# Taking thinned neighbours out by indirect writes into ranked rows, in a two-layer graph kernel

## The chip, the cores and the metric
One core of a Trainium2 chip runs the whole program. The time is device microseconds of that core, lower is better. TensorE, VectorE, ScalarE, GpSimd (POOL in the profile) and SyncE (SP, which here only issues DMAs) each follow their own instruction list and meet at semaphores.

## The reference, cut to what matters
```python
# x (16, 1024, 64) f32, adj (16, 1024, 1024) f32, sparse with heavy hubs; nodemask all true
h = relu(layernorm(x));  x = x + (adj / clip(adj.sum(2), 1)) @ h          # layer 0
h = relu(layernorm(x))                                                    # layer 1
neigh = (adj > 0) & ~eye;  nb = neigh.sum(-1)
rank = cumsum(neigh, -1) - neigh                       # which neighbour of its row
skip = where(nb > 10, (nb + 1) // 2, 1)
rem = neigh & (skip > 1) & (rank % skip == skip - 1) & mask[:, :, None]
rem = rem | rem.T                                      # taken out on both sides
nd = where(eye, 1, adj) with rem set to 0, > 0;  nv = nd.sum(2)
s = sort(where(nd[..., None], h[:, None], inf), axis=2)
agg = sum of w * (quantile tau of the nv sorted values), tau in (.25, .5, .75)
x = x + (relu((h + agg) @ W1 + b1) @ W2 + b2) * mask
```
A row with more than ten neighbours loses at most two of them (the neighbours of rank skip-1 and 2*skip-1), and each loss is taken over into the neighbour's own row. In the inputs that the reference draws, each of the 16 graphs has 44 to 52 nodes with more than ten neighbours, and the largest node has 78.

## The kernel before, in words
The 16 graphs go in 8 pairs (g, b). For each graph the kernel

- streams the transposed adjacency in eight pieces (`adl`, tile AT, ring of 3), makes 0/1 masks of it on VectorE (`nei`, NEIT) and multiplies it for layer 0 on TensorE (`msg`, psL, line 557);
- counts neighbours by matmuls with a triangular matrix (`cum`, line 568) and writes a signed rank code per entry into VR on ScalarE (line 841): for a neighbour a small positive number, for a non-neighbour a negative one. VR is one buffer of eight 128-row tiles, so the next graph's codes wait until this graph's rows have left it;
- thins (`thin` on POOL, `abs` on ScalarE, `rem` on VectorE): POOL works out two target ranks for every row, ScalarE writes |code - middle| into RM (line 848), VectorE turns it into -4096 where it hits a target (line 1169);
- adds VR, RM and RM transposed in PSUM (`sc`, function `codes`, lines 589 to 596), and ScalarE writes the sum through Relu back into VR (line 867): an entry that was taken out becomes 0. ScalarE then counts the row's valid entries by the sum of signs (`cn`, line 873);
- sorts the nodes by neighbour count (`cls`, `key`) and writes each VR row with its features to its rank's place in `rows` in device memory (`sca`, 8 indirect DMAs by POOL, line 1505).

For each pair it then reads the ranked rows back in tiles of 128 (`ldr`, tile RR), turns them (`pos`, `turn`, tiles POSA and POSB), makes one-hot matrices on VectorE (`gd`, OHB, lines 1194 to 1209), gathers the neighbours' features on TensorE (`gm`, psG, lines 651 and 660), sorts them on VectorE (`cmp` on W, `bat` on HUB, lines 1227 to 1277; for HUB ScalarE moves a share), weighs and adds them, and does the two dense products (`f1`, `f2`) and the output (`out`, 16 indirect DMAs). Ranks 0 to 127 are the hubs.

The order in which all this is issued is a string, ORDER, one letter per step kind; each engine walks the same list of steps and does its part of each. A step's place in the string so sets its place in every engine's queue. Graphs with a node of more neighbours than its slots hold go a slow way (`ov`), which is skipped where a flag is 0.

Of the kernel before, what the change touches and what calls it, by code (L numbers as in the profile page):

```python
# [28 lines left out]
    "XnnnUUUAAMMUWUMMAADDRMDDAUUUADDDDMDAAMWDDDTDDDUDMDDRUUMATABBBBBMUBBBMrANAgrrrrrrrNNMUssckWUssssAccss"  # L29
    "cSSSSRMssssccssUUsASMsccDDDSSSMAAhDlDMDWRDDDDDDDNNNDDDDDXThnBBnUUUTnBBBAAgMUBrBBArrrrrrMMrssUcksssAf"  # L30
    "UcssMcscsssscsssWScSSSRsAccMLMDDAUUAASSSSDDFLDUDDDWDDDDDMDDDDDTTFFMRLLBBBBFrrBFFgUUBBBMMLLMFFrrArrrr"
    "fksFAssssssssslddsVVAccmNmddNccmmvdNdUMeWLULsmmSAevdUdAUmdGmdeeFFFLLmdsSommccesdhSSFFmSRddsKKKKsKKcc"
    "MAFMDDlDDDLUDKLSSSMDDDAAmmWDDDDeeTKddQBBMKBBmmDRUUUKDDDDdmNQrdQdeFTFBFBLLNBBmmtXQQdFFQQmFgrrrerQLLQr"
    "rrANssssssdndcenmknsssSssAFFFQWcccttMMptssscmUepssUMMdAcdcmmSSQScAUAtDDQSSSSpDLLDDRtdAdDDDmmtMDteUUt"
    "FFFeLLMtpUAAMMtWFFFpLDLDDDDJJpRJFFFTUUAMJJGtDADDDThtBMBadUBdffMlABBBBBULLMrmmrNrrddmderrrrFmQUFQtFms"
    "AesgddtssAssLssLNkccccWmsssQQNVVAtmdshSmeesQSSSddRtstQsvMQtMtttttttsttUtcUccpmmMAAddcMlSQQpFFSSSFeRm"
    "UUXUDDDDDQDmQQWDDDDDDQQNDddANNDEDDLLmmTDDeddeETEnvmmddFFEnAmmgtBBoFnderkdEAEMmMBBBBBBrrrrErmEeLUrrUL"
    "sssesssccKKKKKKMMcsssssdcdEFFFpcmUSSSSssssWRttAMAtcLLscmpMcUAttKMUDDSSStSMAAUDDDeFFFELLKddQWKKmDDDDD"
    "DDDEFQRQDDtFFQQDDDdmQQdmTmTtUQQBBhBAUAlLLBBMUFFFBrBBNrQAgQMrMrQtrrrrLLQeeUUFFFNtJMOkssssssJLLpOssJNJ"
    "ssssccJddcQtsmmQteQSSdccmWdSSmASAAdGGdRtsmmchcQddpttDDDMDQtttUAUttssAtcMMMQtSSStDtlWRetfefpmtttmpXeF"  # L40
# [1630 lines left out]
```

## Time and profile before
| | |
|---|---|
| median of 3 runs | 1417.88 us (1410.16, 1417.88, 1423.46) |
| span of the profiled execution | 1381.6 us |
| TensorE matmul busy | 1209.3 us, 88% |
| VectorE busy | 1129.0 us, 82% |
| ScalarE busy | 958.9 us, 69% |
| GpSimd busy | 734.6 us, 53% |

The profiled execution's own time is not shown beside its span; the span lies 28.6 us below the fastest of the three runs and 36.3 us below their median. An engine's busy time is the sum of its instructions, and what is left of the span is time in which it waited.

### The profile page before, as it was taken

To read this page: it belongs to the slowest core of one execution; us is meant where nothing else is said; L and a number is where in the kernel's file an instruction comes from. 1 tells how busy PE (TensorE), PEld (TensorE's weight loads), DVE (VectorE), ACT (ScalarE), POOL (GpSimd) and SP (SyncE) were. 2 spreads that over 40 slices of the span, in tenths; PEclk is the share of its full clock that TensorE was granted. 3 is DMA by queue.
4 is the path that set the end of the run, shared out by engine and by line. 5 is a ranking of instruction groups with operands and counts; after the bars stand their busy time and mean duration, and the time that the engine had idled before them with its cause. 6 is when DMAs were issued, how large, how long until landed. Compare 5 with 4: busy or idle time off the path is not lost.

```text
span 1381.6 us, 32444 instructions
## 1 busy us (share of the span) xinstructions
PE 1209.3 (88%) x12833; PEld 893.1 (65%) x12833; DVE 1129.0 (82%) x2060; ACT 958.9 (69%) x1755; POOL 734.6 (53%) x988
## 2 busy tenths in 40 slices
PE   4979999999899989999999989899898999688543
PEld 4757776867577676667767667667666676555221
DVE  3441379989899889999799989889897999888980
ACT  1787778887789678888678677777775888743311
POOL 0463434454558753876547665774477553721325
PEclk9988799999999999999799998999898999889655
DMA  4355543554245433535444433446134341331000
GB/s 136 130 161 181 157 140 107 196 176 145 83 156 159 141 113 102 159 115 171 126 135 138 135 109 112 140 136 208 52 116 125 103 141 46 133 87 36 8 9 15
DMA packets 119032, 167.08 MB, mean 121 GB/s; under 512 B 58816, under 2 KB 59472, under 8 KB 118864
## 3 DMA queue, kind: packets, MB, share of 16 engines
q1 hardware_dynamic: 103168, 117.72, 28.9%
q0 software_dynamic: 14336, 46.42, 8.8%
q8 instruction: 101, 1.65, 0.5%
q10 hardware_dynamic: 1360, 0.74, 0.2%
q14 instruction: 67, 0.55, 0.1%
HBM read 114.25 MB, written 50.59 MB: 119 GB/s over the span
## 4 chain that ended last, share of the span: by engine, by line
PE 42%; DVE 23%; POOL 14%; issue 8%; ACT 7%; DMA 4%; ACTq 1%; SPq 0%; POOLq 0%; DVEq 0%
PE psL L557 11%; PE psG L660 6%; PE psT L568 5%; POOL out L1546 5%; PE psG L651 4%; DVE HUB L1276 4%; DVE HUB L1277 4%; PE psM L706 3%; DVE OHB L1209 3%; PE psT L589 2%; POOL rows L1505 2%; PE psT L593 2%; PE psT L604 2%; PE psT L596 2%; DVE OHB L1194 2%
## 5 line engine op out<-in xcount | busy, mean ns | idle before, releaser
L557 PE MATMUL psL<-H0A,AT 128*128 128x65 f32 x2048 | 274.3, 296 | 12.4 <-issue 8.6
L557 PEld LDWEIGHTS psL<-H0A,AT 128*128 128x128 f32 x2048 | 266.3, 212 | 24.3 <-issue 21.1
L1505 POOL DMA_INDIRECT rows<-VR,IDX x128 | 171.1, 1336 | 87.3 <-ACT JUNK L873 48.0
L1276 DVE TENSOR_TENSOR HUB<-HUB 128x1472 f32<-128x1472 f32 (+6 forms) x224 | 184.8, 825 | 11.9 <-ACT HUB L984 9.0
L1277 DVE TENSOR_TENSOR HUB<-HUB 128x1472 f32<-128x1472 f32 (+6 forms) x224 | 188.6, 842 | 0.0
L568 PE MATMUL psT<-UM,NEIT 128*128 128x512 f16 (+3 forms) x1024 | 161.0, 306 | 21.0 <-ACT VR L841 11.3
L867 ACT ACTIVATE VR<-psT 128x512 f16<-128x512 f32 x256 | 149.1, 598 | 43.4 <-PE psT L596 33.3
L660 PE MATMUL psG<-OHB,HL 128*64 128x384 f16 (+5 forms) x2048 | 170.2, 316 | 9.3 <-DVE OHB L1209 4.2
L1546 POOL DMA_INDIRECT out<-FR x128 | 154.5, 1207 | 38.4 <-issue 36.3
L651 PE MATMUL psG<-OHB,HL 128*64 128x256 f16 (+1 forms) x2560 | 152.9, 279 | 6.9 <-ACT HUB L952 3.7
L848 ACT ACTIVATE RM<-VR,SK 128x1024 f16<-128x1024 f16 x128 | 138.0, 1151 | 20.2 <-POOL SK L1456 20.2
L651 PEld LDWEIGHTS psG<-OHB,HL 128*64 128x64 f16 x2560 | 137.0, 116 | 19.9 <-DVE OHB L1194 8.9
L568 PEld LDWEIGHTS psT<-UM,NEIT 128*128 128x128 f16 x1024 | 88.8, 101 | 88.6 <-ACT VR L841 15.0
L660 PEld LDWEIGHTS psG<-OHB,HL 128*64 128x64 f16 x2048 | 106.7, 111 | 58.9 <-issue 9.1
L984 ACT ACTIVATE HUB<-HUB 128x1472 f32<-128x1472 f32 (+5 forms) x168 | 90.7, 540 | 69.5 <-DVE HUB L1277 67.8
L873 ACT ACTIVATE JUNK<-VR 128x1024 int8<-128x1024 f16 x128 | 134.4, 1058 | 0.1
L1163 DVE TENSOR_SCALAR NEIT<-AT 128x1024 f16<-128x1024 f32 x128 | 90.8, 730 | 30.7 <-DMA AT<-in_adjt 30.7
L593 PEld LDWEIGHTS psT<-CH,RM 128*128 128x128 f16 x1024 | 83.7, 100 | 48.9 <-issue 4.6
L841 ACT ACTIVATE VR<-psT,CF 128x512 f16<-128x512 f32 x128 | 80.7, 697 | 46.9 <-PE psT L568 41.9
L589 PE MATMUL psT<-VR,CH 128*128 128x512 f16 x256 | 100.6, 393 | 10.3 <-DVE RM L1169 6.2
L593 PE MATMUL psT<-CH,RM 128*128 128x128 f16 x1024 | 107.3, 223 | 0.0
L841 ACT ACTIVATE VR<-psT,CB 128x512 f16<-128x512 f32 x128 | 79.7, 692 | 32.7 <-POOL CB L1426 16.7
(135 smaller groups left out, 2273.0 us busy)
## 6 DMA issues: line engine op xcount, KB each, us to landing
AT<-in_adjt SPq DMA_DIRECT2D x128, 512.0 KB, 4.7
RR<-rows SPq DMA_DIRECT2D x128, 288.0 KB
FR<-rows SPq DMA_DIRECT2D x16, 272.0 KB, 4.7
X<-in_x SPq DMA_DIRECT2D x16, 256.0 KB, 3.7
h<-VR SPq DMA_DIRECT2D x16, 256.0 KB
rows<-VR,IDX POOLq DMA_INDIRECT x128, 4.3
out<-FR POOLq DMA_INDIRECT x128
CH<-in_ch ACTq DMA_DIRECT2D x1, 192.0 KB, 4.5
```

The lines of the kernel that those rows point to most:

```text
L557: m = e.matmul(ps["L"][:, 65 * t:65 * t + 65], AT[:, n % RING, kk, t * P:t * P + P], H0A[:, T * b + 2 * kp + kk, :], start=(kp == kk == t ...
L568: m = e.matmul(o[:, kk * P:COLS], half(t // 4)[:, at:at + P], UM[:, 0:COLS - kk * P], start=(kk == 0), stop=(kk == 3), skip_group_check=True)
L593: e.matmul(oj, RM[:, t, k * P:k * P + P], idh, start=False, stop=False, skip_group_check=True)
L651: m = e.matmul(bk[C * b:C * b + C, at:at + cols], HL[:, part, (2 * g + b) % 3, k, :], OHB[:, n % 2, b, k * cols:k * cols + cols], start=(k ...
L660: m = e.matmul(bk[C * b:C * b + C, 0:cols], HL[:, part, (2 * g + b) % 3, k, :], OHB[:, n % 2, b, kk * cols:kk * cols + cols], start=(k == ...
L841: e.activation(VR[:, t, COLS * ch:COLS * ch + COLS], t_bank(u), ACT.Identity, bias=bias).then_inc(t_empty, 1)
L848: e.activation(RM[:, t, :], VR[:, t, 0:N], ACT.Abs, bias=SK[:, 3, t:t + 1]).then_inc(a_abs, 1)
L867: e.activation(VR[:, k, 512 * ch:512 * ch + 512], t_bank(u), ACT.Relu).then_inc(t_empty, 1)
L1276: e.tensor_tensor(b0, a0, a1, ALU.max)
L1277: e.tensor_tensor(b1, a0, a1, ALU.min).then_inc(v_bat, 1)
L1505: e.indirect_dma_start(row_d[:, :], bass.IndirectOffsetOnAxis(ap=IDX[:, gb % 2, t:t + 1], axis=0), VR[:, t, :].bitcast(I32), None).then_in ...
L1546: e.indirect_dma_start(out_d, bass.IndirectOffsetOnAxis(ap=dst, axis=0), fr[:, rt, 0:2 * C].bitcast(F32), None).then_inc(d_out[g % 2], 16)
```

## The change
The rank codes in VR are written to `rows` as they are, with 2 more columns per row (a dump place for writes that have no target). The steps `abs`, `rem` and `sc` are gone. In their place, once a graph's eight scatters have landed, SP stores the node-to-rank table (`ranks`), and loads the 128 hub rows into HB (step `hub`). POOL works out the two target ranks of each hub row (`thin`, now on 128 rows instead of 1024), VectorE finds the two columns with MAX_INDEX (`find`), POOL reads the ranks of those two neighbours from `ranks` by two indirect DMAs, writes -1 over the hub's own two entries by two more (`rank`), and over the hub's entry in the two neighbours' rows by another two (`take`). Each such DMA moves 128 elements. The row loads (`ldr`) wait for the last two. The valid count `cn` is now taken from RR after the load, of codes that may be negative, and becomes a count by `0.5 * sum + 513`. A row of rank 128 or more with more than ten neighbours sets a flag for the slow way. The class limit 10 of the sorting becomes 11. `rows` is one tensor per graph, with rows of 2580 instead of 2576 bytes. ORDER is new throughout. Its first two lines and the parts of the code that count:

```diff
 ORDER = (
-    "XnnnUUUAAMMUWUMMAADDRMDDAUUUADDDDMDAAMWDDDTDDDUDMDDRUUMATABBBBBMUBBBMrANAgrrrrrrrNNMUssckWUssssAccss"
-    "cSSSSRMssssccssUUsASMsccDDDSSSMAAhDlDMDWRDDDDDDDNNNDDDDDXThnBBnUUUTnBBBAAgMUBrBBArrrrrrMMrssUcksssAf"
...
+    "nnMnMAXAMMAWARAUAUDDDUMMDDDAUADMDDUWADDDDDMDDUUUDDRMUUUUNgNAAMUWMNkMUDDSSDSAMDSSDMUDDDSSMSAWUURAAMhA"
+    "DDlRDADDNDDNTDHgXUNBiUADDkSSUSMAMMUSnMMMhnDSSSUSrHcWTDDDnBrADMMWAARFDDiMRADMUULUDDDUAUDlDcALLDDFAFNL"
...
         for k in range(T):
-            for ch in range(2):
-                add("s", "sc", g, b, k, ch)
-            add("c", "cn", g, b, k)
             add("S", "sca", g, b, k)
+        for c, kind in (("H", "hub"), ("T", "thin"), ("i", "find"), ("B", "rank"), ("r", "take")):
+            add(c, kind, g, b)
...
+                    e.dma_start(rank_d[gb].rearrange("(t p) o -> p (t o)", p=P), IDX[:, gb % 2, :], allow_slow_non_contiguous=True).then_inc(d_rt, 16)
+                elif kind == "hub":
...
+                    for t in range(T):
+                        w.wait_ge(d_sca[t], 16 * (gb + 1))
+                    if gb:
+                        w.wait_ge(v_find, gb)
+                        w.wait_ge(o_adr, gb)
+                    e.dma_start(HB[:, :].bitcast(I32), rows(g, b)[0:P, :]).then_inc(d_hub, 16)
                 elif kind == "ldr":
...
-                    for t in range(T):
-                        w.wait_ge(d_sca[t], 16 * (2 * g + b + 1))
+                    w.wait_ge(d_gone[b], 32 * (g + 1))
...
-            def codes(g, b, k, ch):
-                w.wait_ge(v_rem, T * (2 * g + b + 1))
-                o = t_free("sc", g, b, k, ch)
-                e.matmul(o, idh, VR[:, k, 512 * ch:512 * ch + 512], start=True, stop=False, skip_group_check=True)
-                for j in range(4):
-                    t = 4 * ch + j
-                    oj = o[:, j * P:j * P + P]
-                    e.matmul(oj, RM[:, t, k * P:k * P + P], idh, start=False, stop=False, skip_group_check=True)
-                    if t == k:
-                        e.matmul(oj, CH[:, CH_4K, :], idh, start=False, stop=False, skip_group_check=True)
-                e.matmul(o, idh, RM[:, k, 512 * ch:512 * ch + 512], start=False, stop=True,
-                         skip_group_check=True).then_inc(t_full, 1)
...
-            def distance(g, b, t):
...
-                e.activation(RM[:, t, :], VR[:, t, 0:N], ACT.Abs, bias=SK[:, 3, t:t + 1]).then_inc(a_abs, 1)
...
-            def coded(g, b, k, ch):
...
-                e.activation(VR[:, k, 512 * ch:512 * ch + 512], t_bank(u), ACT.Relu).then_inc(t_empty, 1)
...
+            def valid(g, b, rt):
...
+                e.activation(JUNK[:, n % 2, :], RR[:, n % 2, 0:N], ACT.Sign,
+                             accum_out=NV[:, T * b + rt:T * b + rt + 1]).then_inc(a_cn, 1)
...
-            def removed(g, b, t):
...
-                e.tensor_scalar(rm, rm, SK[:, 4, t:t + 1], -4096.0, ALU.is_equal, ALU.mult).then_inc(v_rem, 1)
+            def find(g, b):
...
+                w.wait_ge(d_hub, 16 * (gb + 1))
+                w.wait_ge(o_thin, gb + 1)
...
+                e.max_index(FOUND[:, :], NW[:, :], HB[:, 0:N]).then_inc(v_find, 1)
...
+            def targets(g, b):
...
+                w.wait_ge(v_find, gb + 1)
...
+                w.wait_ge(d_rt, 16 * (gb + 1))
+                for q in range(2):
+                    e.indirect_dma_start(RK[:, q:q + 1], None, rank_d[gb][:, :],
+                                         bass.IndirectOffsetOnAxis(ap=JI[:, q:q + 1], axis=0)).then_inc(d_rk, 16)
...
+                for q in range(2):
+                    e.indirect_dma_start(flat(gb), bass.IndirectOffsetOnAxis(ap=ADR[:, q:q + 1], axis=0),
+                                         GONE[:, :], None).then_inc(d_own, 16)
...
+            def take_out(g, b):
...
+                w.wait_ge(d_rk, 32 * (gb + 1))
...
+                w.wait_ge(d_own, 32 * (gb + 1))
+                for q in range(2):
+                    e.indirect_dma_start(flat(gb), bass.IndirectOffsetOnAxis(ap=ADR[:, 2 + q:3 + q], axis=0),
+                                         GONE[:, :], None).then_inc(d_gone[b], 16)
```

How the new order moves things is seen at three places. On TensorE, after the first graph's rank matmuls (UM, NEIT), before the change the code matmuls (VR, CH and RM) begin and the sorting matmuls (GE) stand among them:

```order
L557 MATMUL psL<-H0A,AT 128x65 [waits d_adj2]
L557 MATMUL psL<-H0A,AT 128x65 x7
L589 MATMUL psT<-VR,CH 128x512 [waits t_empty,v_rem]
L593 MATMUL psT<-CH,RM 128x128
L595 MATMUL psT<-CH 128x128
L593 MATMUL psT<-CH,RM 128x128 x3
L596 MATMUL psT<-RM,CH 128x512
L589 MATMUL psT<-VR,CH 128x512 [waits t_empty]
L593 MATMUL psT<-CH,RM 128x128 x4
L596 MATMUL psT<-RM,CH 128x512
L576 MATMUL psT<-GE,CH 128x128 [waits t_empty,o_cls]
```

and now, at the same place, after the same products:

```order
L584 MATMUL psL<-H0A,AT 128x65 [waits d_adj1]
L584 MATMUL psL<-H0A,AT 128x65 x7
L603 MATMUL psT<-GE,CH 128x128 [waits t_empty,o_cls]
L605 MATMUL psT<-GE,UM 128x112
...
L610 MATMUL psT<-GE,CH 128x128
L584 MATMUL psL<-H0A,AT 128x65 [waits d_adj2]
L584 MATMUL psL<-H0A,AT 128x65 x7
L595 MATMUL psT<-UM,NEIT 128x512 [waits t_empty,v_nei,o_diag]
```

The code matmuls are gone, and the next graph's rank matmuls follow on the sort directly. On POOL, for the second graph of the first pair, the new chain stands as one block behind `thin`:

```order
L1501 TENSOR_SCALAR HSK<-HSK,HB 128x2
L1512 CAST AT<-FOUND 128x2 [waits o_in,v_find]
...
L1522 DMA RK<-ranks,JI 128x1 [waits d_rt,o_ji]
L1522 DMA RK<-ranks,JI 128x1
...
L1533 DMA rows<-GONE,ADR 1320960x1 [waits o_in]
L1533 DMA rows<-GONE,ADR 1320960x1
L1543 CAST AT<-RK 128x2 [waits d_rk]
...
L1555 DMA rows<-GONE,ADR 1320960x1 [waits d_own,o_adr]
L1555 DMA rows<-GONE,ADR 1320960x1
L1480 TENSOR_SCALAR CB<-VR 128x4 [waits t_empty]
```

Six indirect DMAs and their three waits come ahead of the next graph's carry (CB). For other graphs the scatters of the next graph stand between the third and fourth and the last two.

On VectorE, for the last graph of all, the rank (PLACE, RS) of which the scatters' index is made, and the search for its hub rows:

```order
L1211 TENSOR_REDUCE RS<-PLACE 128x8 [waits v_in]
...
L1225 TENSOR_SCALAR OHB<-POSA 128x4096 [waits p_gm]
L1283 TENSOR_TENSOR W<-W,psS 128x384 [waits p_cr]
L1236 TENSOR_SCALAR OHB<-POSA 128x2x640 [waits p_gm]
L1307 TENSOR_TENSOR HUB<-HUB 128x4x368 [waits v_bat]
...
L1263 TENSOR_TENSOR W<-W 128x112 [waits v_in]
L1283 TENSOR_TENSOR W<-W,psS 128x384 [waits p_cr]
L1200 MAX_INDEX FOUND<-NW,HB 128x8 [waits o_ji,o_thin,d_hub]
L1236 TENSOR_SCALAR OHB<-POSA 128x2x640 [waits p_gm]
L1307 TENSOR_TENSOR HUB<-HUB 128x1472 [waits a_bat,v_bat]
```

Nineteen VectorE instructions of the pair before stand between the two, among them five pairs of HUB steps (L1307, L1308): two of 1472 elements, two of 736 and one of 1104; behind the search the same sort goes on.

## Rows read from the trace of the kernel before

**Rows 1.** The page, section 1: busy time, share of the span, instructions
```profile
span 1381.6 us, 32444 instructions
PE 1209.3 (88%) x12833; PEld 893.1 (65%) x12833; DVE 1129.0 (82%) x2060; ACT 958.9 (69%) x1755; POOL 734.6 (53%) x988
```

**Rows 2.** Windows, three stretches: length, busy us of each engine, PEclk, DMA share
```profile
0.00:200.00 200.00, 167.95 (x1376) 134.37 (x1377) 77.95 (x147) 132.33 (x222) 75.88 (x149) 0.90 0.48 150
200.00:1300.00 1100.00, 1006.69 (x11181) 741.49 (x11179) 1008.62 (x1833) 810.51 (x1496) 631.53 (x812) 0.95 0.39 124
1300.00:1381.60 81.60, 34.64 (x278) 17.26 (x278) 42.47 (x82) 16.06 (x39) 27.23 (x27) 0.57 0.03 11
```

**Rows 3.** VectorE's waits, 200 to 1300 us: total us, times, longest
```profile
DVE W L1252 <- PE psS L693: 15.1, 13, 5.3
...
DVE OHB L1209 <- PE psG L651: 6.2, 4, 3.3
```

**Rows 4.** VectorE's waits, 0 to 200 us
```profile
DVE ST L1149 <- PE psL L557: 27.3, 5, 10.4
DVE PLACE L1178 <- ACT AHEAD L855: 20.1, 3, 10.0
```

**Rows 5.** Groups by shape that the change removes: busy us, mean ns, idle before
```profile
L867 ACT ACTIVATE VR<-psT 128x512 f16<-128x512 f32 x256 | 149.1, 598 | 43.4 <-PE psT L596 33.3
L848 ACT ACTIVATE RM<-VR,SK 128x1024 f16<-128x1024 f16 x128 | 138.0, 1151 | 20.2 <-POOL SK L1456 20.2
L593 PE MATMUL psT<-CH,RM 128*128 128x128 f16 x1024 | 107.3, 223 | 0.0
L589 PE MATMUL psT<-VR,CH 128*128 128x512 f16 x256 | 100.6, 393 | 10.3 <-DVE RM L1169 6.2 <-ACT VR L867 2.9 <-ACT AHEAD L855 0.9
L596 PE MATMUL psT<-RM,CH 128*128 128x512 f16 x256 | 99.4, 388 | 0.0
L1169 DVE TENSOR_SCALAR RM<-RM,SK 128x1024 f16<-128x1024 f16 x128 | 64.8, 556 | 11.0 <-ACT RM L848 8.3 <-issue 2.7
L595 PE MATMUL psT<-CH 128*128 128x128 f16 x128 | 28.7, 224 | 0.0
```

**Rows 6.** The same view: nearest rows to what is added, and a sorting step
```profile
L1505 POOL DMA_INDIRECT rows<-VR,IDX x128 | 171.1, 1336 | 87.3 <-ACT JUNK L873 48.0 <-issue 27.8 <-DVE VR L1111 10.6
L1276 DVE TENSOR_TENSOR HUB<-HUB 128x1472 f32<-128x1472 f32 x32 | 58.6, 1831 | 1.8 <-ACT HUB L984 1.6
L1105 DVE TENSOR_REDUCE ST<-H0A 128x16 f32<-128x1024 f32 x8 | 9.7, 1213 | 1.4 <-ACT H0A L827 1.4
```

**Rows 7.** DMA queues, and issues with KB and median us to landing
```profile
q1 hardware_dynamic: 103168, 117.72, 28.9%
...
FR<-rows SPq DMA_DIRECT2D x16, 272.0 KB, 4.7
rows<-VR,IDX POOLq DMA_INDIRECT x128, 4.3
```

**Rows 8.** Windows of 40 us, columns as in rows 2
```profile
0.00:40.00 40.00, 22.29 (x116) 20.05 (x116) 11.56 (x20) 7.29 (x11) 3.22 (x8) 1.00 0.47 137
80.00:120.00 40.00, 30.63 (x210) 24.24 (x209) 16.46 (x33) 28.08 (x45) 20.18 (x43) 0.74 0.47 147
1320.00:1360.00 40.00, 19.21 (x78) 7.57 (x74) 23.87 (x55) 7.55 (x19) 12.06 (x12) 0.53 0.03 8
```

**Rows 9.** Timeline, POOL and VectorE, first two graphs: start us, us, [idle before]
```profile
54.64 0.23 POOL L1456 TENSOR_SCALAR SK<-SK 128x4 f32<-128x4 f32 x1
82.14 1.30 POOL L1505 DMA_INDIRECT rows<-VR,IDX  x1 [0.30 <-issue]
115.03 0.61 POOL L1480 TENSOR_SCALAR IDX<-RS 128x8 int32<-128x8 f32 x1 [14.03 <-DVE RS L1180]
130.26 0.96 POOL L1505 DMA_INDIRECT rows<-VR,IDX  x1 [0.30 <-issue]
162.98 1.85 DVE L1205 TENSOR_SCALAR OHB<-POSA 128x3072 f16<-128x3072 f16 x2
```

More of the change, by code:

```diff
@@ L146, in merge_stages, with halvings @@
         p *= 2
+def halvings(n):
+    return [(p, k) for p, k in merge_stages(n)]
 def stage_views(x, p, k):
@@ L205, in prepare @@
                 add("D", "cum", g, b, t, 1)
-            add("T", "thin", g, b, hf)
-            for t in range(4 * hf, 4 * hf + 4):
-                add("B", "abs", g, b, t)
-                add("r", "rem", g, b, t)
         for part in range(3):
@@ L224, in fill @@
                 add("L", "ldr", g, b, rt)
+                add("c", "cn", g, b, rt)
                 add("F", "pos", g, b, rt)
@@ L405, in program @@
         d_sca = [sem(f"d_sca{t}") for t in range(T)]
+        d_hub, d_rt, d_rk, d_own = (sem(n) for n in ("d_hub", "d_rt", "d_rk", "d_own"))
+        d_gone = [sem(f"d_gone{i}") for i in range(2)]
         d_adj = [sem(f"d_adj{i}") for i in range(RING)]
@@ L633, in flags @@
                         m = e.matmul(o[0:32, j * P:j * P + P], FLC[:, b, 4 * ch + j:4 * ch + j + 1].to_broadcast([P, 32]),
-                                     idh, start=(j == 0 and b == 0), stop=(j == 3 and b == 1), skip_group_check=True)
+                                     idh, start=(j == 0 and b == 0), stop=False, skip_group_check=True)
+                for b in range(2):
+                    m = e.matmul(o[0:32, :], FLO[:, b:b + 1].to_broadcast([P, 32]),
+                                 UM[:, P:P + 1].to_broadcast([P, COLS]), start=False, stop=(b == 1), skip_group_check=True)
                 m.then_inc(t_full, 1)
@@ L1479, in index @@
                 w.wait_ge(v_rank, gb + 1)
-                e.tensor_scalar(IDX[:, gb % 2, :], RS[:, :], float(N * gb), None, ALU.add).then_inc(o_idx, 1)
+                if gb >= 2:
+                    w.wait_ge(d_rt, 16 * (gb - 1))
+                    for t in range(T):
+                        w.wait_ge(d_sca[t], 16 * (gb - 1))
+                e.tensor_copy(IDX[:, gb % 2, :], RS[:, :]).then_inc(o_idx, 1)
             def update(g, b, t0):
@@ L1556, in gpsimd @@
                     thin(*a)
+                elif kind == "rank":
+                    targets(*a)
+                elif kind == "take":
+                    take_out(*a)
                 elif kind == "cls":
@@ L1618, in constants @@
     cf[:, CF_DST:CF_DST + T] = n
+    for q in range(2):
+        cf[:, CF_DUMP + q] = ROW * d + R_DUMP + q
+        cf[:, CF_BACK + q] = -(ROW * d + R_DUMP + q)
+        cf[:, CF_SKIP + q] = -(R_DUMP + q)
+    cf[:, CF_HALF] = N / 2 + 1
     cap = np.zeros(N)
```

340 lines of the change are left out of this document (216 added, 124 removed).

## The prediction
> **What bounds the kernel now.** I read the page's busy times first [rows 1]: TensorE works 1209.3 us of 1381.6 and VectorE 1129.0; ScalarE (958.9) and POOL (734.6) are well below. A share over the whole span hides stages, so next the windows [rows 2]. In the 1100 us from 200 to 1300, TensorE is busy 1006.7 and VectorE 1008.6: two engines at 92%, each filling the other's pauses badly. The three stretches give VectorE's idle time as 122 us in the first 200, 91 in the middle, and 39 in the last 82. Last, whom VectorE waits for: in the middle first of all TensorE (15.1 for psS, 6.2 for psG, with smaller ones some 30 of the 91) [rows 3]; at the start the message sums on TensorE, 27.3, and AHEAD on ScalarE, 20.1, both queued among the code steps [rows 4]. So the kernel is bound by two engines of nearly the same load, with a start of its own.
>
> **What is removed.** TensorE: the code matmuls are 107.3 + 100.6 + 99.4 + 28.7 = 336.0 us [rows 5], which leaves 1209.3 - 336.0 = 873. ScalarE: 149.1 (Relu) + 138.0 (distance) = 287.1, which leaves 672; the sign count moves, at the same 128 instructions of one row length. VectorE: 64.8 for the target mask [rows 5]. POOL: 32 runs of `thin` with 11 small instructions each.
>
> **What is added.**
> - VectorE: 16 MAX_INDEX over 1024 columns. No row shows it. Below, a reduce over 1024 elements takes 1213 ns [rows 6]; above, I allow two such passes, 2.4 us. I take 1.2, since each column has to be read once: 16 x 1.2 = 19 (up to 39). VectorE's work becomes 1129.0 - 64.8 + 19 = 1083.
> - POOL: 6 indirect DMAs per graph, 96 in all. A scatter of whole rows costs 1336 ns [rows 6] and 0.96 when nothing disturbs it [rows 9], so 92 to 128 us. Small instructions stay about even: 22 of `thin` go per graph, 22 of the chain and 2 in the sort come, at 0.23 to 0.61 us [rows 9]. With 115 us more POOL stands at 850, under VectorE's 1083, even with ten microseconds of waiting for landings per graph (160).
> - SP: per graph one load of 128 hub rows (like the FR load, 4.7 us to landing [rows 7]) and the table store, 1024 pieces of 4 bytes. A packet of queue q1, mostly far larger, takes 28.9% of 16 x 1381.6 us over 103168, 62 ns [rows 7]. So the store holds the 16 engines for up to about 4 us, 64 in all, where they are 39% busy [rows 2]. I cost it at nothing; its cover is the adjacency ring of three, and if a store and a hub load together delay an adjacency piece by more than that, VectorE's first wait of rows 4 comes back in the middle.
> - The landing chain. The row loads now wait, after the last scatter has landed, for: hub load 4.7, search 1.2, 22 small POOL instructions at 0.3 (6.6), six issues at 1.3 (8), and two landings that nothing covers at 4.3 each [rows 7, 9], 29 us; at 0.61 per small instruction 36. What it replaces in the first graph is the way from the end of `thin` at 54.9 to the last scatter at 83.4 [rows 9], 28.5 us, most of it codes. Only the sort and the scatters of it remain.
>
> **Where the chain lies.** In the middle each graph has some 68 us (1100 over 16) to cover it. What is queued behind it: on SP the hub load waits for eight scatters with adjacency loads behind; on POOL the waits for the search and for two landings have the next graph's carry and diagonal behind them, on which ScalarE's and TensorE's rank steps hang; on VectorE the search waits for SP and POOL with everything behind. The last is the one that can cost the bound. From RS to the search these must pass: index 0.6, eight scatters 10.4, landing 4.3, hub load 4.7, seven small instructions of `thin` 2.3, 22 to 24 us. In the order the last graph has, in between, one-hots and weights of about 4 and five HUB pairs of 13.5 (2 x 1.831 us per 1472 elements [rows 6], the others by their elements), 18 us: 5 us short. By the same count the first graph of each pair has 29 to 77 us of cover and the second 13 to 27. I add 10 us to the middle for this, some 2 for each second graph that is short. At the start there is no pair to cover it. The second graph's index came 14 us after POOL was ready for it (115.03, idle 14.03), since AHEAD stood behind the codes; that goes, and about as much for the first graph. The last scatter (131.2 before) thus moves some 20 to 25 us forward, and the chain takes 29 back. The first one-hot at 163 [rows 9] therefore stays within 10 us either way. What I do take off the start is 8 us of the 47 that VectorE waited for TensorE and AHEAD, the rest being chain: 122 becomes 114.
>
> **The sum.** Once TensorE has 873 us of work against 1083, VectorE alone is the bound. Its span is work plus idle: 1083 + 114 (start) + 55 (middle, of which 10 from the search) + 39 (end) = 1291. The middle's 91 could stay (other engines' latency) or go to about 20 (in-order waits never all go); I take half and those 10, because TensorE and the issue order of two full engines made about that much. The end is the last pair's sort and output, which the change doesn't touch. The runs' median lies 36.3 above the span of the profile shown, so 1291 + 36 = **1327 us**, 6% less.
>
> **TensorE's clock.** The rows show that a less busy TensorE gets a lower granted clock: 0.95 in the middle at 92% busy; 0.74 in 80 to 120 us at 77%, 0.53 at 48% near the end, where most of the time goes at the lower level, 1.2 GHz; but also 1.00 at 56% in the first 40 [rows 2, 8]. In the new kernel it would be 873 of 1291, 68% busy.
> The Trainium skill, TensorE: Matmul & The Clock Gate (Part 1: The HAM clock gate), says half rate is the default and only sustained activity lifts it. By that rule the removal of matmuls gives a part of its gain back, and the trace agrees except in the first 40 us. It is a rival below.
>
> **The rivals.**
> 1. *The pauses stay.* The new waits (hub load, search, landings) make as much idle time as TensorE's relief takes away. For it: each engine is in order, and three engines wait in the new chain. Against: TensorE loses 28% and ScalarE 30% of its work. 1083 + 122 + 91 + 39 = 1335, + 36 = 1371. Chance 0.14.
> 2. *The clock falls.* At a clock of 0.77 (as in 80 to 120) instead of 0.92, 873 us become at most 1040, 80% of the span: TensorE's waits on VectorE's path stay, 91 in the middle, with the start at 114: 1363. Only under about 0.67 would TensorE (1190) be the bound again. Chance 0.10.
> 3. *VectorE without pauses.* Middle idle 20, start 95: 1083 + 95 + 20 + 39 = 1237, + 36 = 1273. Chance 0.08.
> 4. *Slower: the search stops VectorE.* MAX_INDEX stands in VectorE's queue where the scatters, the hub load and `thin` aren't done. If POOL and SP come to their part late, by as much as landing 4.3 + load 4.7 + seven small instructions 2.3 in every graph, that is 16 x 11.3 = 181 us: 1327 + 181 = 1508. It decides from (1418 - 1327) / 16 = 5.7 us per graph. For it: it is the one step where VectorE, the bound, waits for two queues, and the cover of second graphs is short. Against: first graphs have cover to spare. Chance 0.05.
> 5. *The slow way is taken*, so that the kernel doesn't do what it says: a row of rank 128 or more with over ten neighbours sets the flag, and then 896 rows go one by one. The drawn graphs have 44 to 52 such nodes, sorted ahead of the rest, so it isn't. Chance 0.01; many times slower.
>
> **How the numbers follow.** The forecast, 1290 to 1352, has the remaining 0.62. The range runs from rival 3 to a little above rival 1, where MAX_INDEX costs double (20 more, half of it hidden): **1272 to 1382**; outside are the slow rivals (0.06) and some 0.05 beyond each mechanism's own size. A measurement of this kernel can't tell 1% from no change, so faster means under 1403.7: 0.62 + 0.14 + 0.10 + 0.08 less 0.02 for tails, 0.92. Within 1%: 0.03. Slower: 0.05.
>
> **What will show it.** Right: VectorE busy near 1083 and TensorE near 873 (more if its clock falls); VectorE about 95% busy in the middle, its waits for psS and psG shorter; first one-hot between 153 and 173 us; MAX_INDEX near 1.2 us with little idle before it; POOL near 850. Wrong: idle time before MAX_INDEX or before the adjacency masks in the middle (rivals 4 and 1), a granted clock under 0.8 in the middle with VectorE waiting for TensorE (rival 2), POOL steps over 1.5 us per issue or waits on the last two writes before RR loads that reach TensorE's turns.

## The result, and the profile after

The changed kernel takes **1545.72 us** (median of four, 1536.2 to 1558.19) where the kernel before took 1420.22 in the same session: a ratio of 1.092, 95% interval 1.084 to 1.100. It is slower; I had forecast 1327 us and a 5% chance of slower. The profile before is of an execution some 36 us faster than the median and the one after of one 12 us slower, so of the 175 us between the two spans only 125 are the change's.

The page's first section of the kernel after (busy us, share of the span, instructions), against [rows 1]:

```profile
span 1556.4 us, 29038 instructions
PE 1153.5 (74%) x11201; PEld 841.7 (54%) x11201; DVE 1082.6 (70%) x1964; ACT 692.1 (44%) x1371; POOL 829.8 (53%) x1120
```

VectorE has the work that I had worked out (1083) and POOL a little less than my 850. TensorE has 1153.5 where I had 873. No engine is above 74%: VectorE stands idle for 473.8 us where it was 252.6. The windows, as in [rows 2]:

```profile
0.00:200.00 200.00, 136.48 (x1037) 114.17 (x1037) 71.74 (x132) 60.37 (x105) 81.66 (x149) 0.83 0.54 151
200.00:1300.00 1100.00, 877.80 (x8744) 638.74 (x8745) 837.09 (x1531) 544.09 (x1085) 640.29 (x865) 0.86 0.44 120
1300.00:1460.00 160.00, 96.54 (x1103) 67.47 (x1101) 120.94 (x210) 67.72 (x139) 66.50 (x71) 0.72 0.24 58
1460.00:1556.00 96.00, 42.67 (x320) 21.30 (x320) 52.85 (x93) 19.95 (x43) 41.36 (x37) 0.55 0.04 12
```

VectorE is idle 263 us in the middle 1100 where it was 91, and TensorE's granted clock there is 0.86, not 0.95. VectorE's waits over the whole span (total, times, longest):

```profile
DVE NEIT L1191 <- DMA AT<-in_adjt: 79.0, 22, 18.9
DVE HUB L1307 <- ACT HUB L991: 61.9, 23, 10.9
DVE ST L1177 <- PE psL L584: 49.1, 13, 11.8
DVE W L1283 <- PE psS L710: 44.1, 17, 10.0
DVE FOUND L1200 <- issue: 18.3, 4, 11.5
```

Before, the wait for adjacency pieces and ScalarE's for the scatters (after: 93.4, 14, 17.1) were:

```profile
DVE NEIT L1163 <- DMA AT<-in_adjt: 30.7, 8, 8.6
ACT VR L841 <- DMA rows<-VR,IDX: 4.7, 6, 1.5
```

The 30.7 lay wholly in the first 200 us. This is the wait that the prediction calls VectorE's first wait of [rows 4], though those rows don't show it; it was to come back in the middle if a table store and a hub load delay a piece by more than the ring covers. It did: of the 79.0, 26.1 lie between 200 and 1300. The last of the five is the search, my slow rival: with 7.2 more from POOL some 25 us, not the 181 of that rival. The timeline shows how the first wait comes about (start, us, what; the queue's rows run from issue to landing):

```profile
104.87 0.38 SPq L540 DMA_DIRECT2D ranks<-IDX  x1
105.66 1.45 POOL L1613 DMA_INDIRECT rows<-VR,IDX  x1 [0.81 <-POOL IDX L1589]
110.08 13.01 SPq L519 DMA_DIRECT2D AT<-in_adjt  x3
125.16 0.69 DVE L1191 TENSOR_SCALAR NEIT<-AT 128x1024 f16<-128x1024 f32 x1 [18.91 <-DMA AT<-in_adjt]
```

The store of a rank table is issued at 104.87, the next adjacency pieces, issued at 110.08, have landed 15 us later, and VectorE stands for 18.91. Steps of the chain of waits in which a scatter or an adjacency load is behind a store (start, us):

```profile
62.67 14.51 DMA rows<-VR,IDX
110.08 15.06 DMA AT<-in_adjt
187.74 13.10 DMA rows<-VR,IDX
329.51 15.88 DMA rows<-VR,IDX
```

A scatter took 4.3 us to land in the median before [rows 7]. Eleven scatters of 9 to 16 us stand in this chain, each issued within 11 us of a table store. ScalarE's wait for scatters, the 93.4 us, is what VR's next graph begins with.

### The profile page after: what moved, and what is told of

Its sections match the earlier page's. It is cut to its first block, busy times and chain, and to the rows that moved or that the text cites. A ratio compares the mean times of both kernels' runs of the same rounds, so it can differ in the third digit from the quotient of the medians.

```text
span 1556.4 us, 29038 instructions
## 1 busy us (share of the span) xinstructions
PE 1153.5 (74%) x11201; PEld 841.7 (54%) x11201; DVE 1082.6 (70%) x1964; ACT 692.1 (44%) x1371; POOL 829.8 (53%) x1120
## 4 chain that ended last, share of the span: by engine, by line
POOL 26%; PE 22%; DVE 16%; DMA 15%; issue 14%; ACT 5%; another core or an unknown queue 2%; ACTq 0%; POOLq 0%; SPq 0%; DVEq 0%
DMA rows<-VR,IDX 9%; PE psL L584 7%; POOL out L1655 5%; POOL rows L1613 5%; PE psG L677 4%; PE psT L595 3%; PE psG L668 2%; DMA AT<-in_adjt 2%; DVE HUB L1307 2%; DVE HUB L1308 2%; PE psM L723 2%; DVE OHB L1225 2%; PE psT L618 1%; DVE OHB L1236 1%
## 5 line engine op out<-in xcount | busy, mean ns | idle before, releaser
L584 PE MATMUL psL<-H0A,AT 128*128 128x65 f32 x2048 | 300.2, 310 | 41.1 <-DMA AT<-in_adjt 16.9
L584 PEld LDWEIGHTS psL<-H0A,AT 128*128 128x128 f32 x2048 | 287.5, 225 | 61.0 <-issue 41.4
L1307 DVE TENSOR_TENSOR HUB<-HUB 128x1472 f32<-128x1472 f32 (+6 forms) x224 | 184.2, 822 | 78.3 <-ACT HUB L991 61.9
L595 PE MATMUL psT<-UM,NEIT 128*128 128x512 f16 (+3 forms) x1024 | 187.6, 324 | 51.3 <-ACT VR L856 29.2
L677 PE MATMUL psG<-OHB,HL 128*64 128x384 f16 (+5 forms) x2048 | 196.5, 340 | 35.5 <-DVE OHB L1236 20.6
L1308 DVE TENSOR_TENSOR HUB<-HUB 128x1472 f32<-128x1472 f32 (+6 forms) x224 | 181.9, 812 | 0.0
L595 PEld LDWEIGHTS psT<-UM,NEIT 128*128 128x128 f16 x1024 | 93.4, 106 | 137.3 <-issue 41.9
L879 ACT ACTIVATE JUNK<-RR 128x1024 int8<-128x1024 f16 x128 | 135.6, 1062 | 29.3 <-DMA RR<-rows 28.8
L618 PE MATMUL psT<-CH,RR 128*128 128x128 f16 x1024 | 88.3, 239 | 55.6 <-DMA RR<-rows 36.2
L723 PE MATMUL psM<-W,CF 128*128 128x384 f32 (+4 forms) x192 | 85.6, 556 | 42.8 <-DVE W L1283 30.6
L618 PEld LDWEIGHTS psT<-CH,RR 128*128 128x128 f16 x1024 | 70.8, 109 | 74.3 <-DMA RR<-rows 38.6
L1236 DVE TENSOR_SCALAR OHB<-POSA 128x3072 f16<-128x3072 f16 (+5 forms) x128 | 90.9, 734 | 23.8 <-ACT Z L898 8.8
L890 ACT ACTIVATE POSA<-psT 128x1024 f16<-128x1024 f16 x80 | 80.9, 1026 | 57.5 <-PE psT L618 47.2
```

The source lines that it names most:

```text
L584: m = e.matmul(ps["L"][:, 65 * t:65 * t + 65], AT[:, n % RING, kk, t * P:t * P + P], H0A[:, T * b + 2 * kp + kk, :], start=(kp == kk == t ...
L595: m = e.matmul(o[:, kk * P:COLS], half(t // 4)[:, at:at + P], UM[:, 0:COLS - kk * P], start=(kk == 0), stop=(kk == 3), skip_group_check=True)
L618: m = e.transpose(o[:, k * P:k * P + P], RR[:, n % 2, k * P:k * P + P], idh)
L677: m = e.matmul(bk[C * b:C * b + C, 0:cols], HL[:, part, (2 * g + b) % 3, k, :], OHB[:, n % 2, b, kk * cols:kk * cols + cols], start=(k == ...
L723: m = e.matmul(ps["M"][:, 0:nn], idf, WA[blk][:, FINAL[blk][d], 0:nn], start=(d == 0), stop=(d == last), skip_group_check=True)
L879: e.activation(JUNK[:, n % 2, :], RR[:, n % 2, 0:N], ACT.Sign, accum_out=NV[:, T * b + rt:T * b + rt + 1]).then_inc(a_cn, 1)
```

## The experiments

All ratios are to the kernel before on the same chip in the same session, with 95% intervals; that kernel took 1376 to 1441 us by chip, so absolute times are compared only within a group. One kernel's ratio moved by 0.017 between two chips (e6 and e18 below), so ratios of different chips are compared no finer than that. e1 to e4 ran on one chip, e5 to e8 on a second, e9 to e12 on a third, e13 to e15 on a fourth and e16 to e18 on a fifth. "The short table" means 32-byte pieces from here on.

### The table store: e1 to e4

`e1_table32` is the changed kernel with the ranks stored partition by partition, eight to a piece, and five more small POOL instructions for the address in the lookup:

```diff
-e.dma_start(rank_d[gb].rearrange("(t p) o -> p (t o)", p=P), IDX[:, gb % 2, :], allow_slow_non_contiguous=True)
+e.dma_start(rank_d[gb].rearrange("(p t) o -> p (t o)", p=P), IDX[:, gb % 2, :])
```

> The changed kernel, with its node-to-rank table laid out so that each partition writes its eight ranks as one piece of 32 bytes (128 pieces instead of 1024); POOL does five more small instructions per graph to turn a node number into the table's address. Theory A (the table store fills the DMA engines: scatters and adjacency loads behind a store land in 9 to 15 us instead of 4 to 5): some 9 us per graph come back, 16 x 9 = 144, so 1546 becomes about 1400, and the first scatters of the first graph land in about 5 us instead of 14.5. Theory B (the search and the hub chain hold the queues of SP, POOL and VectorE): at most 20 us change, 1525 to 1550. Theory C (rows of 2580 bytes scatter slowly): no change, 1546.

Measured 1.035 (1.028 to 1.042): some 80 us come back, half of what theory A named. `e2_before_table4` and `e3_before_table32` are the kernel before with nothing but such a store added, which nothing reads:

```diff
+elif kind == "key":
+    w.wait_ge(o_idx, gb + 1)
+    e.dma_start(rank_d[gb]..., IDX[:, gb % 2, :]).then_inc(d_rt, 16)   # pieces of 4 bytes (e2) or 32 (e3)
```

> The kernel before, with only the table store of the changed kernel added: 1024 pieces of 4 bytes per graph, on SP at the rank step, read by nobody. Theory A: each store holds the DMA engines for about 10 us and stops the scatters and the adjacency loads behind it, so 1420 becomes 1500 to 1570. Theories B and C: the store costs nothing that shows, under 1430.

> As the run before, the same store at the same place with the same wait on SP, but in 128 pieces of 32 bytes. Theory A: 1420 to 1435, since only the count of pieces costs. If instead SP's wait for the index is what costs, it is as slow as the store in 1024 pieces.

Measured 1.062 (1.053 to 1.071) and 1.015 (1.006 to 1.024). `e4_pitch2592` changes the length of a row in memory:

> The changed kernel with rows of 2592 bytes (a multiple of 32) instead of 2580, the added columns unused. Theory C (rows that begin at odd multiples of 4 bytes scatter slowly): about 1450. Theories A and B: 1540 to 1555, nothing or a trifle more for the wider rows.

Measured 1.086 (1.075 to 1.097), the changed kernel's own value, so the row's length is not a cause.

**What follows.** The pieces of 4 bytes cost 0.057 of the ratio in the new kernel (1.092 - 1.035; 0.051 against e4, which ran beside e1) and 0.047 in the old one (1.062 - 1.015). This is shown twice. In 32-byte pieces the store, with SP's wait for it, still costs 0.015 there. Queue q1 of the old kernel, first with pieces of 4 bytes, then of 32 (packets, MB, share of 16 engines):

```profile
q1 hardware_dynamic: 119808, 117.79, 30.3%
```

```profile
q1 hardware_dynamic: 105472, 117.79, 27.7%
```

The spans are 1523.4 and 1438.3 us, so q1 holds the 16 engines for 462 and 398: 63 us for 14336 packets more, and the time grew by 74. That looks like my "4 us per store, 64 in all", but it isn't the same thing. In the traces' packet records the 4-byte packets of q1 take 7 to 9 ns each, 7.4 of the 63 us (10.3 against 2.9). The other 56 are packets of other transfers, which take longer. The loss is a stall behind the store, not the store's own work. Two windows of 8 us that begin 2 us behind a store, of the kernel after and of e1 (the last two columns are DMA share and GB/s):

```profile
107.00:115.00 8.00, 8.00 (x40) 8.00 (x39) 0.00 (x0) 0.00 (x0) 5.91 (x7) 0.50 0.99 49
101.00:109.00 8.00, 8.00 (x40) 8.00 (x39) 0.94 (x1) 0.00 (x0) 6.03 (x7) 0.50 0.77 254
```

Over the 16 stores such a window moves 26 GB/s in the median in the kernel after and 22 in e2, but 252 in e1 and 150 in e3. In the window shown the engines' share is 0.99 and they move a fifth of what they move in e1; behind the first store (59.6 to 69.0 us) the share is 0.27, at 21 GB/s. So the share doesn't tell. Why pieces of 4 bytes do this isn't shown. In the new kernel with the short table, the place of the 18.91 us reads:

```profile
99.07 0.36 SPq L540 DMA_DIRECT2D ranks<-IDX  x1
101.80 7.20 SPq L519 DMA_DIRECT2D AT<-in_adjt  x3
106.77 0.94 DVE L1191 TENSOR_SCALAR NEIT<-AT 128x1024 f16<-128x1024 f32 x1 [8.79 <-DMA AT<-in_adjt]
```

The three pieces take 7.20 us in place of 13.01. Over the whole span VectorE's wait for adjacency is 42.1 us in e1 (41.0 in e6 below, which has no store, so the small pieces' part of the 79.0 is some 37), and 65.3 in e2 against 34.0 in e3; ScalarE's wait for scatters falls from 93.4 to 35.0 in e1.

### The removal and the chain, piece by piece: e5 to e8

Edits, each on the kernel named:

```diff
 e5_before_bare (on before): the code steps and their waits
-                w.wait_ge(v_rem, T * (2 * g + b + 1))
+                return                        # codes; so too distance, Relu copy, comparison; thin stays
 e6_after_bare (on e1): no table, no hub load, no chain
-w.wait_ge(d_gone[b], 32 * (g + 1))             # row loads
+for t in range(T): w.wait_ge(d_sca[t], 16 * (2 * g + b + 1))
 e7_hub_only (on e6): the short table and the hub row load put back
 e8_elsewhere (on e1): the four small writes go to a tensor of its own, the row loads wait as in e6
-return row_d[gb][:, :].rearrange("n (f o) -> (n f) o", o=1)
+return dump_d[gb][:, :].rearrange("n (f o) -> (n f) o", o=1)
```

> The kernel before with the codes taken out and nothing put in: no distance activation, no comparison, no code matmuls or transposes, no Relu copy; the order of the other steps stays the old one. It leaves the thinning out, so more neighbours stay in. Theory P (the removed work was worth what the prediction said, and the chain that replaces it eats it): about 0.92 to 0.94 of before (1320 to 1350 us). Theory Q (the codes lay beside other work, and taking them out is worth little, since the group times of TensorE overlap): 0.97 to 1.00.

> The changed kernel with neither the rank tables nor any step of the chain (no hub row load, no search, no lookups, no small writes; the loads of rows wait for the scatters instead). It leaves the thinning out. Beside the kernel before without codes it differs by the new order and where ranks are counted. Theory P (chain at fault): about the same as that kernel, 0.92 to 0.95. Theory O (the new order itself is the loss): near the changed kernel with short tables, 1.02 to 1.04, while the old order without codes is at 0.93. Theory Q: both 0.97 to 1.00.

> The changed kernel with tables in 32-byte pieces and the load of the hub rows (with its wait for eight scatters ahead of the adjacency loads on the same queue), but no search, lookups or small writes; the loads of rows wait for the scatters. It leaves the thinning out. If the queue's wait in order is the cost, this is near the full chain (1.02 to 1.035); if the lookups, the small writes and the wait for them are, it is near the one without any of it, plus 0.015 for the table.

> The changed kernel with tables in 32-byte pieces and the whole chain, but the small writes go to the same addresses of tensors of their own, so the loads of rows need not wait for them; it leaves the thinning out of the rows that are read. If the latency of the chain in front of the loads is what costs, this falls to about 0.98 to 1.00 of before; if the work and the transfers of the chain on the engines and queues cost, it stays at 1.03.

Measured: e5 0.969 (0.960 to 0.978), e6 0.976 (0.968 to 0.983), e7 0.985 (0.978 to 0.993), e8 1.038 (1.029 to 1.047).

**What follows.** Theory P falls in its first half. Without any replacement the removal is worth 3%, not the 6% of my sum with the chain in it (theory Q said 0.97 to 1.00). The new order isn't to blame: e5 and e6 overlap. The table and the hub load of e7 add 0.009, with overlapping intervals. The wait of the row loads for the last writes isn't the main price: e8, in which they don't wait, is 0.062 over e6 on the same chip. e1 ran on another chip, so a share of up to some 0.02 for that wait isn't excluded. What costs is what the chain does on its way. All of e5 to e8 leave the thinning out of the result. The windows of e5, as in [rows 2]:

```profile
0.00:200.00 200.00, 160.02 (x1219) 133.30 (x1221) 81.06 (x157) 90.13 (x163) 86.04 (x166) 0.85 0.53 163
200.00:1300.00 1100.00, 900.42 (x9930) 666.04 (x9926) 987.33 (x1763) 593.72 (x1202) 620.74 (x805) 0.89 0.39 122
1300.00:1343.00 43.00, 11.32 (x24) 3.59 (x24) 8.72 (x15) 3.90 (x6) 17.91 (x18) 0.50 0.04 13
```

VectorE's idle time is 119 at the start, 113 in the middle and 34 at the end, against 122, 91 and 39 before. The codes went and the pauses stayed. In the middle VectorE waits for TensorE more than before, 46.7 us in all against 31.9: TensorE is busy 1071.8 us here and VectorE 1077.1, so two engines of equal load still wait for each other.

### Which piece of the chain: e9 to e12

All on e1, with what is left out in words: e9 without `targets` and `take_out` (search only), e10 without the six indirect DMAs, e11 without `max_index`, and e12 with nothing but the six DMAs at constant addresses.

```diff
-e.max_index(FOUND[:, :], NW[:, :], HB[:, 0:N]).then_inc(v_find, 1)    # e11; found columns are constants
```

> The kernel with tables in 32-byte pieces and the hub row load, and of the chain only thin and the search on VectorE: no lookups, no target arithmetic, no small writes (the thinning is left out). The kernel with the hub load alone stood at 0.985 of before and the one with the whole chain at 1.035. Theory S (VectorE's wait and work in the search is the cost): at least 1.02. Theory G (POOL's long stretch of small steps and issues, which the carry, the diagonal and the scatters stand behind, is the cost): 0.99 to 1.00, the search being 19.5 us of VectorE.

> As the whole chain with tables in 32-byte pieces, but without its six indirect DMAs per graph; the search and all small arithmetic on POOL stay, and the loads of rows wait for the scatters (the thinning is left out). Theory G with cost by POOL's time: about half of the step from 0.985 to 1.035, since the six issues hold 120 us of POOL and the arithmetic about 130: 1.005 to 1.02. If the indirect DMAs (their transfers, or their landings that POOL waits for) are the cost, 0.99 to 1.00. Theory S: 1.02 or more.

> As the whole chain with tables in 32-byte pieces, but without the search on VectorE: the found columns are constants, so POOL and VectorE do not wait for each other there (other neighbours are taken out than should be). Theory S: 0.99 to 1.00. Theory G: 1.01 to 1.03, since POOL does all it did.

> As the kernel with the hub load alone, plus the six indirect DMAs per graph at their places, to constant addresses of the pad columns, with their waits and the loads of rows behind them; no search and no small arithmetic (the thinning is left out). Theory G by POOL's time: 1.00 to 1.015. If the indirect DMAs are the whole cost: 1.03. If only arithmetic is: 0.985 to 0.99.

Measured: e9 1.002 (0.998 to 1.006), e10 1.018 (1.013 to 1.023), e11 1.052 (1.046 to 1.057), e12 0.993 (0.990 to 0.997).

**What follows.** From the hub load (0.985, e7) to the whole chain (1.035 to 1.038, on other chips than these four) thin and search add 0.017, the target arithmetic 0.016 on those, and the DMAs on top of all that another 0.02. The six DMAs alone add 0.008, which the intervals don't separate from nothing. Theory S (the search is the price) falls as the main price by e11: without the search the ratio is still 1.052. What the search itself costs e11 can't say, since the whole chain wasn't run on that chip. e11 is slower than e1 and e8 by as much as ratios move between chips, and its addresses are others too (all lookups go to the entries of two fixed columns); which of the two it is stays open. e11 and e12 both lie outside what theory G had named for them. POOL's busy time alone isn't the price either: it is 608, 644, 712 and 763 us in e7, e9, e12 and e10, and e12 is faster than e9. The engine that all pieces pass is POOL. A stretch of its timeline in e1, from the end of eight scatters to the next graph's diagonal:

```profile
710.06 1.02 POOL L1628 DMA_INDIRECT rows<-VR,IDX  x1 [0.30 <-issue]
719.82 0.29 POOL L1496 TENSOR_SCALAR HSK<-HB 128x1 f32<-128x1 f32 x1 [8.73 <-DMA HB<-rows]
...
732.77 1.50 POOL L1537 DMA_INDIRECT RK<-ranks,JI  x1 [0.29 <-issue]
...
739.28 2.17 POOL L1548 DMA_INDIRECT rows<-GONE,ADR  x1 [0.28 <-POOL ADR L1545]
...
746.56 1.53 POOL L1566 CAST ADR<-AT 128x2 int32<-128x2 f32 x1
748.37 1.03 POOL L1570 DMA_INDIRECT rows<-GONE,ADR  x1 [0.28 <-POOL ADR L1566]
749.71 0.98 POOL L1570 DMA_INDIRECT rows<-GONE,ADR  x1 [0.31 <-issue]
750.72 1.16 POOL L1479 TENSOR_TENSOR NEIT<-NEIT,CH 128x512 f16<-128x512 f16 x1
```

POOL waits 8.73 us for the hub rows and reaches the diagonal, on which TensorE's rank matmuls hang, 31 us later. 24 of these are the chain, the rest other work between its parts. The 128x2 cast of 1.53 us takes 0.18 where VectorE stands idle (at 117.19 in the kernel after); that VectorE's idleness is the reason isn't shown.

### The place in POOL's order, and TensorE's part: e13 to e18

```diff
 e13_later (on e1), POOL's own order only
+(0, "rank") behind ("cls", g, 1); (0, "take") behind the last scatter of (g, 1)
+(1, "rank"), (1, "take") behind ("off", g + 1, 0, 1)
 e16_sort_first (on e1): only the pair's first graph, both behind ("cls", g, 1)
 in e13 and e16 a step moves only where its old place was earlier (e16: five of eight "rank", three "take")
 e15_thin_vector (on e13): thin's eight instructions in VectorE's find, ahead of max_index
 e14_twice (on e5)
-for kk in range(4):
+for kk in (0, 1, 2, 3, 0, 1, 2, 3):
 e17_table32_again is e1 and e18_bare_again is e6, beside e16
```

> The changed kernel with tables in 32-byte pieces, all its work and its result, but on POOL alone the two long pieces of the chain stand later: for the first graph of a pair the lookups behind the sort's classes of the second and the last writes behind its scatters, for the second graph both behind the next pair's carry and diagonal. If the chain costs by what stands behind it in POOL's order, this falls from 1.035 to about 1.00 to 1.015. If it costs by its amount, or by its landings, it stays at 1.03 or more.

> The kernel before without the codes, with the rank matmuls (256 groups of four) done twice, the first time for nothing: TensorE alone has about 130 to 190 us more of group time, no engine waits for anything new. (The thinning is left out.) If the lower clock took the codes' gain back, the clock rises from 0.872 towards 0.91 and the time stays at 0.965 to 0.975 or falls. If the work on TensorE counts as such, 0.99 to 1.00. If TensorE has room to spare and the clock does not matter, 0.97 at an unchanged clock.

> As the one with the later places on POOL, and the eight small instructions of thin are issued on VectorE ahead of its search, which then waits for the hub rows alone. VectorE gets 128 small instructions of about 0.1 us, 13 us; POOL loses about 35 us. If the chain costs by POOL's amount of work and by the search waiting for POOL: 0.01 less than the same kernel with thin on POOL. If VectorE is what bounds: 0.01 more.

> The changed kernel with tables in 32-byte pieces, all its work and its result; on POOL alone, the lookups and writes of each pair's first graph stand behind the sort's classes of the second graph instead of ahead of them, where POOL waits for VectorE's sort anyway; the second graph's chain stays. If what stands behind the chain is its price, this is 0.005 to 0.02 under the kernel with the old places beside it. If the late writes, for which the queue with the row and adjacency loads waits, are the price, it is the same or up to 0.02 over it.

> The same kernel as the changed one with tables in 32-byte pieces, measured again on the chip of the next two: 1.03 to 1.04 as before if the ratio does not depend on the chip.

> The same kernel as the changed one without tables and chain, measured again (the thinning is left out): 0.97 to 0.985 as before if the ratio does not depend on the chip, and the price of hub load, chain and short tables together is then 0.05 to 0.065 of before.

Measured: e13 1.067 (1.059 to 1.075), e15 1.071 (1.063 to 1.078) and e14 1.012 (1.004 to 1.020) on one chip; e16 1.061 (1.055 to 1.067), e17 1.032 (1.024 to 1.039) and e18 0.959 (0.955 to 0.964) on another.

**What follows.** On one chip the short table, hub load and chain cost 0.072 (e17 less e18), where the second chip has 0.062 (e8 less e6; the loads of e8 don't wait for the last writes). This is the price of the replacement, and it is shown twice. The page of e18, then e17:

```profile
PE 1109.6 (81%) x11201; PEld 813.2 (59%) x11201; DVE 1074.6 (79%) x1932; ACT 690.6 (50%) x1371; POOL 605.2 (44%) x672
```

```profile
PE 1139.4 (77%) x11201; PEld 830.0 (56%) x11201; DVE 1089.1 (74%) x1964; ACT 692.9 (47%) x1371; POOL 855.8 (58%) x1200
```

POOL does 250.6 us more in 528 instructions; VectorE 14.5 more. Waits of ScalarE and TensorE in e18, then in e17:

```profile
ACT VR L852 <- POOL CB L1483: 40.5, 13, 11.5
...
PE psT L591 <- POOL NEIT L1475: 9.1, 3, 4.4
PE psT L614 <- DMA RR<-rows: 2.0, 3, 1.2
```

```profile
ACT VR L856 <- POOL CB L1487: 78.6, 17, 14.7
...
PE psT L595 <- POOL NEIT L1479: 20.8, 5, 10.8
PE psT L618 <- DMA RR<-rows: 20.5, 9, 10.3
```

The carry, the diagonal and the row loads are what comes late. But the old places were the best of those tried. (In them the second graph's scatters stand between "rank" and "take" for three graphs only; for most the chain is one block.) With the first graph's chain put behind the second graph's classes and so directly ahead of its index (e16), that graph's scatters and all behind them are later; TensorE's and ScalarE's waits in e16:

```profile
PE psT L595 <- POOL NEIT L1479: 37.4, 5, 14.6
```

```profile
ACT VR L856 <- DMA rows<-VR,IDX: 65.8, 13, 19.5
```

against 20.8 and 41.7 in e17. With everything later (e13) the queue of the loads stands for the last writes:

```profile
SPq L557 <- DMA rows<-GONE,ADR: 148.4, 10, 28.6
```

where e17 has 79.9. e16 is 0.029 over e17, more than the 0.02 that I had named for late writes, and e13 is 0.035 over e1, where I had hoped for a gain. My reading is that it is not one badly chosen place: 250 us of POOL work in an in-order line have work that others wait for on both sides. The waits fit this, but no run shows it alone. One speaks against POOL's amount of work: thin moved to VectorE took 30 us from POOL (850.8 to 821.1) and gave nothing (1.071 against 1.067).

e14 bears on TensorE's part. The doubled rank matmuls add 133 us of busy time (170.5 to 303.1), the granted clock stays at 0.875 to 0.884 (e5: 0.865 to 0.879), and the ratio rises by 0.043, some 60 us. e5 ran on another chip, so this may be 0.03 to 0.06. Work on TensorE then counts at some 0.3 to 0.6 of its time, not at nothing as it would beside one bounding VectorE. The run was meant to lift the clock too and didn't, so it can't say what the lower clock costs.

## Why the prediction was wrong, point by point

Three steps of the prediction failed: the table store costed at nothing, TensorE's work costed at 873 us so that VectorE alone would be the bound, and POOL's chain costed at nothing because POOL's total stays under VectorE's.

- **"I cost it at nothing" (the table store): failed, 0.05 to 0.057 of the loss of 0.092.** I priced a piece of 4 bytes by the mean packet of q1, 62 ns, and so got 4 us per store; its packets took 7 to 9 ns. That the total of q1 grew by 63 us, as my 64 said, is luck: the growth is in the packets of other transfers behind the store, which stall for some 8 us at 22 to 26 GB/s. The cover was wrong too. The middle had a DMA share of 0.39, and I took that as room, but the scatters that VR's next graph waits for and the adjacency pieces are issued within microseconds of the store. Those scatters landed in 9 to 16 us and not in 4.3, and three pieces took 13.0 us and not 7.2. I had named that sign (VectorE's wait for adjacency) under rivals 1 and 4, but no rival has the store as its cause.
- **TensorE "leaves 873": failed as arithmetic.** Busy time after is 1153.5, and 1071.8 in e5, though 336.0 us of groups went. Group times of matmuls overlap, so they don't add up to busy time: all groups of the kernel before add up to 1631.5 us, its busy time is 1209.3. The groups that stay rose from 1295.5 to 1346.7 in e5, so at most some 50 of the 199 us between 873 and 1072 are matmuls that took longer; the rest is overlap.
- **"VectorE alone is the bound", the middle's 91 us going to 45: failed with it.** In e5, without any chain, the middle's idle time was 113, and TensorE was as busy as VectorE, so the condition of the sum never held. My rival 1, the pauses stay, was right for this part. How much of the pauses is this pair of engines and how much the latency of the others isn't settled. The removal is worth 3 to 4% (e5, e18). 65 us less of VectorE's work alone would be 4.6% and with the start's 8 and the middle's 46 8%.
- **"POOL stands at 850, under VectorE's 1083", hence no cost: the number held (829.8), the conclusion failed, 0.06 to 0.07 with the short table and the hub load.** I checked the landing chain against the row loads (68 us of cover) and the search against VectorE, and listed that carry and diagonal stand behind POOL's waits, but priced neither. My 24 us for the chain behind the hub load about held in the stretch shown (24 of 31); what I left out is the work that waits behind it. e17 and e18 show the price and the later carry and diagonal; that POOL's order is the whole of it is argued.
- **The search: right.** 1216 ns against 1.2 us, 25 us of idle time before it against my 10, and e11 shows that it isn't the main price. Rival 4 had the right sign and the wrong place.
- **The clock (rival 2): it fell, from 0.92 to 0.82 and to 0.86 in the middle, less than rival 2 supposed.** (Its 0.77 is the busy share of the row that it names; the clock there is 0.74 [rows 8], by which 873 would be 1085 us.) What it cost is open. The rank matmuls of 512 columns take 391 ns before and 411 in e5. An estimate: the 51 us by which the staying groups grew, at e14's rate of some 0.45, are some 20 us of e5. The Trainium skill, TensorE: Matmul & The Clock Gate (Part 1: The HAM clock gate), says that only sustained activity lifts the clock. This case agrees in direction: 0.917 with TensorE busy 88% of the span, 0.872 at 80% (e5), 0.821 at 74%. e14 (83%) has 0.877.
- **The start:** the first one-hot stands at 170.5 us, within 153 to 173; with the short table it is at 159.2 and without chain at 153.3.

No version made here does all of the work and beats the kernel before. With the chain free, 0.96 to 0.975 is the most that this change gave in the two orders tried.

## What to carry to other kernels

A store in small pieces can cost far more than its packets take, and its cost lies in what is issued just behind it: look at the GB/s and at the loads and scatters of the next microseconds, not at the mean DMA share. Don't subtract group times of matmuls from TensorE's busy time, since they overlap. An engine far under the bound may still set the pace if it works in order: follow what the next item's first steps wait for, and not its total. Before counting on the pauses of the bounding engine to shrink, take the work out and put nothing in; that run costs little and caps the gain.

## What the runs showed of the hardware

- Behind a store of 1024 pieces of 4 bytes the 16 DMA engines moved 22 to 26 GB/s for the 8 us from 2 to 10 us after its issue (medians of 16 stores), against 150 to 252 behind 128 pieces of 32 bytes, though the small packets themselves took 7 to 9 ns each. Scatters behind it landed in 9 to 16 us in place of 4.3. The cost was 0.047 to 0.057 of the time for 16 stores.
- The index search over 128 x 1024 f16 takes VectorE 1216 ns, as a reduce over 1024 elements does [rows 6]:

```profile
L1200 DVE FIND_INDEX8 FOUND<-NW,HB 128x8 uint32<-128x1024 f16 x16 | 19.5, 1216 | 0.0
```

- An indirect DMA of one 2- or 4-byte element per partition costs POOL as much to issue as one of whole rows:

```profile
L1613 POOL DMA_INDIRECT rows<-VR,IDX x128 | 152.5, 1191 | 61.3 <-issue 44.7 <-DVE VR L1139 9.5 <-POOL IDX L1589 6.1
L1533 POOL DMA_INDIRECT rows<-GONE,ADR x32 | 40.3, 1259 | 10.2 <-POOL ADR L1530 5.3 <-issue 4.9
L1522 POOL DMA_INDIRECT RK<-ranks,JI x32 | 38.5, 1204 | 8.4 <-issue 8.4
```

- A small POOL instruction on 128x2 elements took from 0.18 to 1.64 us in the stretches read here.
- The same kernel takes 1376 us on one chip and 1441 on another; the ratio of one change went from 0.976 to 0.959 between two chips.
